# Four score products an item instead of six, in a Macaron layer on one core

## What is computed

```python
x = x + 0.5 * _L0_ffn_ref(_layernorm(x, axis=-1), ...)
x = x + _L0_attn_ref(_layernorm(x, axis=-1), ...)
x = x + 0.5 * _L0_ffn_ref(_layernorm(x, axis=-1), ...)
...
attn = jnp.einsum('bhqd,bhkd->bhqk', q * scale, k)
attn = jnp.where(causal[None, None], attn, -jnp.inf)
attn = jax.nn.softmax(attn, axis=-1)
out = jnp.einsum('bhqk,bhkd->bqhd', attn, v).reshape(b, s, d)
```

## Time and profile before

| | before |
|---|---|
| runs | 1226.78 us median of 3 (1225.18 to 1227.13) |
| profiled execution | 1226.45 us, span in the trace 1224.7 us |
| PE busy | 1165.3 us (95%), weight loads 701.2 us (57%) |
| DVE, ACT, POOL busy | 796.2 (65%), 578.0 (47%), 669.8 us (55%) |
| granted clock of PE | 0.992 of full speed over the span |
| L420, the scores | 192 products, 24.3 us busy |

### The profile page before, as it was taken

The page is one execution under the profiler, slowest core; times in us unless marked ns, Lnnn a source line. Parts: engine busy times, 40 slices in busy tenths (PEclk is TensorE's granted clock), DMA queues, the critical chain, the costliest instruction groups (busy, mean ns, idle before and its releaser), DMA issues.

```text
span 1224.7 us, 22657 instructions
## 1 busy us (share of the span) xinstructions
PE 1165.3 (95%) x8315; PEld 701.2 (57%) x8315; DVE 796.2 (65%) x1571; ACT 578.0 (47%) x954; POOL 669.8 (55%) x740
## 2 busy tenths in 40 slices
PE   4699999998999899999899999899999999999998
PEld 2355555565555566666566566566565565666655
DVE  5688787567866766666766667767567555554444
ACT  3444454343456545555455554554644545333332
POOL 4454334357567766666666677577564546333332
PEclk9799999999999999999999999999999999999999
DMA  6112120000000000000000000000000000000000
GB/s 217 45 56 82 52 65 1 1 1 1 1 1 1 1 1 2 1 1 2 1 2 1 1 1 2 1 18 2 1 2 1 18 1 1 1 10 9 1 1 19
DMA packets 10107, 19.25 MB, mean 16 GB/s; under 512 B 2192, under 2 KB 6800, under 8 KB 10000
## 3 DMA queue, kind: packets, MB, share of 16 engines
q1 hardware_dynamic: 8992, 14.64, 3.7%
q10 hardware_dynamic: 1008, 3.15, 0.7%
HBM read 15.70 MB, written 2.10 MB: 15 GB/s over the span
## 4 chain that ended last, share of the span: by engine, by line
PE 69%; DVE 7%; POOL 3%; issue 2%; ACT 1%; DVEq 0%; ACTq 0%; POOLq 0%
PE YB L297 20%; PE G L278 19%; PE U L278 19%; PE S L420 2%; POOL RR L1067 1%; PE S L446 1%; PE S L461 1%; DVE TS L680 1%; PE S L352 1%; DVE MXN L891 1%; DVE TS L684 1%; ACT TS L509 1%; PE S L392 1%; PE S L396 1%; PE S L398 1%
## 5 line engine op out<-in xcount | busy, mean ns | idle before, releaser
L1011 POOL TENSOR_TENSOR HS<-TS,HS 128x512 f16<-128x512 f32 x256 | 303.1, 1184 | 433.5 <-ACT HS L516 433.1
L680 DVE SCALAR_TENSOR_TENSOR TS<-TS,G 128x512 f32<-128x512 f32 x256 | 175.6, 686 | 372.0 <-ACT TS L509 371.6
L297 PE MATMUL YB<-W,HS 128*128 128x256 f16 x3036 | 374.7, 273 | 20.3 <-DVE X L700 20.3
L278 PE MATMUL G<-XS,W 128*128 128x512 f16 x1536 | 377.5, 382 | 2.9 <-ACT W L523 1.8
L278 PE MATMUL U<-XS,W 128*128 128x512 f16 x1536 | 376.4, 381 | 0.0
L297 PEld LDWEIGHTS YB<-W,HS 128*128 128x128 f16 x3036 | 292.2, 98 | 98.7 <-DVE X L700 29.9
L509 ACT ACTIVATE TS<-G,TSC 128x512 f32<-128x512 f32 x256 | 175.5, 686 | 297.5 <-PE U L278 290.9
L516 ACT ACTIVATE HS<-TS 128x512 f16<-128x512 f32 x256 | 161.2, 630 | 273.8 <-DVE TS L684 268.1
L278 PEld LDWEIGHTS U<-XS,W 128*128 128x128 f16 x1536 | 151.1, 98 | 183.9 <-issue 4.4
L278 PEld LDWEIGHTS G<-XS,W 128*128 128x128 f16 x1536 | 147.6, 98 | 136.4 <-issue 6.4
L684 DVE SCALAR_TENSOR_TENSOR TS<-TS,U 128x512 f32<-128x512 f32 x256 | 175.8, 687 | 8.8
(11 more groups left out here) (160 smaller groups left out, 861.6 us busy)
## 6 DMA issues: line engine op xcount, KB each, us to landing
out_y<-X SPq DMA_DIRECT2D x16, 128.0 KB, 1.7
X<-in_x SPq DMA_DIRECT2D x3, 512.0 KB, 6.1
room<-in_gate SPq DMA_DIRECT2D x3, 512.0 KB, 3.1
room<-in_up SPq DMA_DIRECT2D x3, 512.0 KB, 3.2
room<-in_down SPq DMA_DIRECT2D x3, 512.0 KB, 3.9
QKT<-in_gate SPq DMA_DIRECT2D x3, 512.0 KB, 3.6
QKT<-in_up SPq DMA_DIRECT2D x3, 512.0 KB, 3.7
QKT<-in_down SPq DMA_DIRECT2D x3, 512.0 KB, 4.5
```

Of the source, the lines that this page charges most:

```text
L278: mm = eng.matmul(bank[:, :], W[:, e, wl, jj, kk * I + m * P:kk * I + (m + 1) * P], flat(XS16[:, b % 2, xl, kk, :, :], 'cq'), start=q == 0 ...
L297: mm = eng.matmul(out, HS[:, j % 2, hl, kk, m * P:(m + 1) * P], W[:, e, wl, 2, kk * D:(kk + 1) * D], start=kk + hl + wl == 0, stop=kk == K ...
L680: eng.scalar_tensor_tensor(TS[:, k % 3, :], TS[:, k % 3, :], 1.0, GB[k % 2][:, :], ALU.add, ALU.mult).then_inc(L['v_t'].sem, 1)
L1011: eng.tensor_tensor(HS[:, j % 2, 1, m, :], TS[:, k % 3, :], HS[:, j % 2, 0, m, :], ALU.subtract).then_inc(L['g_lo'].sem, 1)
```

## The change

The scores of an item are laid out anew over the three banks. Before, bank S0 held block a (first keys, first query tile), S1 block b (first keys, second query tile) and S2 block c (second keys, second query tile), each bank filled by both halves of the array, one 256-column product from each; the second product of a bank waited for the first. Now S1 and S0 each take the first keys for both query tiles from one half of the array, a single product of 512 columns each, and only S2 (block c) still takes two products of 256 columns, the second one waiting for the first.

What follows from the layout: blocks a and b now hold both query tiles, and in both the half of the first tile has to be masked. One `pool_mask` does both (a select over 2 x 256 elements a partition, as many as before), and `act_ph` of block b now has to wait for it. `act_ph` b moves from slot s+2 to s+3, and `pool_pl` b from s+3 to s+4. `pe_pv` reads other places of the same blocks, in as many products.

```diff
--- before.py
+++ after.py
@@ -195,7 +195,7 @@
         N_AW = 8
         L = {}
         for name, labels in [
-                ('p_gu', 'gu'), ('p_y', 'y'), ('p_w', 'wt wb'), ('p_lg', 'lg'), ('p_ft', 'tp'), ('p_at', 'tp'), ('p_qt', 'q'), ('p_kt', 'k'), ('p_q2', 'q'), ('p_mx', 'ab'), ('p_qk', 'qkv'), ('p_s0', 'a0 b1 c1'), ('p_sc', 'b a c'), ('p_pv', 'pv'), ('p_op', 'tp mm'),
+                ('p_gu', 'gu'), ('p_y', 'y'), ('p_w', 'wt wb'), ('p_lg', 'lg'), ('p_ft', 'tp'), ('p_at', 'tp'), ('p_qt', 'q'), ('p_kt', 'k'), ('p_q2', 'q'), ('p_mx', 'ab'), ('p_qk', 'qkv'), ('p_s0', 'c0'), ('p_sc', 'b a c'), ('p_pv', 'pv'), ('p_op', 'tp mm'),
                 ('a_t', 'tanh'), ('a_h', 'hi'), ('a_w', 'hi0 hi1 hi2 sc2'), ('a_wq', 'hi'), ('a_fx', 'xh'), ('a_fc', 'xs'), ('a_ac', 'xt'), ('a_qc', 'q'), ('a_kc', 'k'), ('a_q2', 'q'), ('a_rx', 'ex'), ('a_ax', 'xh'), ('a_e', 'b a c'), ('a_ph', 'b a c'), ('a_qh', 'qhi khi0 khi1'), ('a_ot', 'ot'),
                 ('v_t', 't'), ('v_h', 'h'), ('v_y', 'y'), ('v_mx', 'mx0 mx1 mx2'), ('v_wr', 'wr dg'), ('v_sc', 'cl pe rc tsc gu cf sc'), ('v_lo', 'lo0 lo1'), ('v_wq', 'cl pe rc qs sc lo'),
                 ('v_fst', 'stats'), ('v_fag', 'aggr'), ('v_fep', 'eps'), ('v_fx', 'xn'), ('v_ls', 'ls mx sub'), ('v_rp', 'sum rc p eq gt'), ('v_wt', 'cum wt'), ('v_wb', 'wtc'), ('v_wc', 'wc'),
@@ -415,19 +415,18 @@
             s2_read(eng, s)
             eng.wait_ge(*L['a_q2'].at(2 * b + 1, 'q'))
 
-            def part(bank, kt, qt, h):
+            def part(bank, kt, qts, h):
+
                 r = slice(64 * h, 64 * h + 64)
-                return eng.matmul(bank[:, h * 2 * P:(h + 1) * 2 * P], qk[r, kt, H // 2 + kv, :], qk[r, qt, 2 * kv:2 * kv + 2, :], start=(bank is S0) == (h == 0), stop=False, skip_group_check=True, tile_position=(64 * h, 0))
-            part(S0, 0, 0, 0).then_inc(L['p_s0'].sem, 1)
-            part(S1, 0, 1, 1).then_inc(L['p_s0'].sem, 1)
-            part(S2, 1, 1, 1).then_inc(L['p_s0'].sem, 1)
-
-            eng.wait_ge(*L['p_s0'].at(i, 'b1'))
-            part(S1, 0, 1, 0).then_inc(lane.sem, 1)
-            eng.wait_ge(*L['p_s0'].at(i, 'a0'))
-            part(S0, 0, 0, 1).then_inc(lane.sem, 1)
-            eng.wait_ge(*L['p_s0'].at(i, 'c1'))
-            part(S2, 1, 1, 0).then_inc(lane.sem, 1)
+                n = len(qts) * 2 * P
+                out = bank[:, 0:n] if kt == 0 else bank[:, h * n:(h + 1) * n]
+                return eng.matmul(out.rearrange('p (t g q) -> p t g q', t=len(qts), g=2), qk[r, kt, H // 2 + kv, :], qk[r, qts[0]:qts[-1] + 1, 2 * kv:2 * kv + 2, :], start=kt == 0 or h == 0, stop=False, skip_group_check=True, tile_position=(64 * h, 0))
+            part(S2, 1, (1,), 0).then_inc(L['p_s0'].sem, 1)
+            part(S1, 0, (0, 1), 1).then_inc(lane.sem, 1)
+            part(S0, 0, (0, 1), 0).then_inc(lane.sem, 1)
+
+            eng.wait_ge(*L['p_s0'].at(i, 'c0'))
+            part(S2, 1, (1,), 1).then_inc(lane.sem, 1)
 
         def pe_pv(eng, i, s):
             bank = (S0, S0, S1, S2)[i % 4]
@@ -439,11 +438,12 @@
             for qt in range(2):
                 for g in range(G):
                     o = bank[:, (qt * G + g) * VW:(qt * G + g + 1) * VW]
-                    terms = [(0, 0)] if qt == 0 else [(1, 0), (2, 1)]
+
+                    terms = [(g % 2, 2 * qt + g // 2, 0)] + [(2, 2 * (g % 2) + g // 2, 1)] * qt
                     q = 0
-                    for blk, kt in terms:
+                    for blk, at, kt in terms:
                         for ph in (PH, PL):
-                            mm = eng.matmul(o, ph[:, blk, g // 2 + g % 2 * 2, :], VS[:, b % 3, kt, kv, :], start=q == 0, stop=q == 2 * len(terms) - 1)
+                            mm = eng.matmul(o, ph[:, blk, at, :], VS[:, b % 3, kt, kv, :], start=q == 0, stop=q == 2 * len(terms) - 1)
                             q += 1
             mm.then_inc(L['p_pv'].sem, 1)
 
@@ -616,9 +616,7 @@
             if c == 'b':
 
                 eng.wait_ge(*L['p_pv'].at(i - 1, 'pv'))
-                eng.wait_ge(*L['a_e'].at(i, 'b'))
-            else:
-                eng.wait_ge(*L['g_mk'].at(i, c))
+            eng.wait_ge(*L['g_mk'].at(i, 'c' if c == 'c' else 'a'))
             eng.activation(flat(PH[:, blk, :, :], 'gk'), flat(P32[:, blk, :, :], 'gk'), ACT.Copy).then_inc(L['a_ph'].sem, 1)
 
         def act_ot(eng, t):
@@ -648,8 +646,8 @@
                 act_exp(eng, i, 'a')
             for i in due(ITEM, s, 2):
                 act_exp(eng, i, 'c')
+            for i in due(ITEM, s, 3):
                 act_ph(eng, i, 'b')
-            for i in due(ITEM, s, 3):
                 act_ph(eng, i, 'a')
             for i in due(ITEM, s, 4):
                 act_ph(eng, i, 'c')
@@ -1095,9 +1093,9 @@
             eng.tensor_copy(vs[:, :, 2 * HD:3 * HD], VR[:, 1, :, :]).then_inc(lane.sem, 1)
 
         def pool_mask(eng, i, c):
-            blk = 'abc'.index(c)
             eng.wait_ge(*L['a_e'].at(i, c))
-            eng.affine_select(out=P32[:, blk, :, :], in_=P32[:, blk, :, :], compare_op=ALU.is_ge, fill=0.0, base=0, pattern=[[0, G], [1, P]], channel_multiplier=-1).then_inc(L['g_mk'].sem, 1)
+            p, pattern = (P32[:, 0:2, 0:2, :], [[0, 2], [0, 2], [1, P]]) if c == 'a' else (P32[:, 2, :, :], [[0, G], [1, P]])
+            eng.affine_select(out=p, in_=p, compare_op=ALU.is_ge, fill=0.0, base=0, pattern=pattern, channel_multiplier=-1).then_inc(L['g_mk'].sem, 1)
 
         def pool_pl(eng, i, c):
             blk = 'abc'.index(c)
@@ -1122,8 +1120,8 @@
                 pool_mask(eng, i, 'a')
             for i in due(ITEM, s, 3):
                 pool_mask(eng, i, 'c')
+            for i in due(ITEM, s, 4):
                 pool_pl(eng, i, 'b')
-            for i in due(ITEM, s, 4):
                 pool_pl(eng, i, 'a')
             for i in due(ITEM, s, 5):
                 pool_pl(eng, i, 'c')
```

## The result

| | before | after |
|---|---|---|
| median | 1226.95 us (1225.18 to 1227.28, 4 runs) | 1234.49 us (1232.10 to 1235.55, 4 runs) |
| ratio | | 1.0067 (95%: 1.0054 to 1.0079), slower |
| profiled execution, span | 1226.45, 1224.7 us | 1232.10, 1230.3 us |
| from the first score product to the end of the span | 1224.7 - 341.8 = 882.9 us | 1230.3 - 339.7 = 890.6 us |

The last line leaves out the start-up, which differs from one execution to the next (the first score product comes at 338.8 to 342.2 us in the fourteen traces of this study); by it the change costs 7.7 us.

A forecast was written before the change was run, and what follows sets the result against it. PE's own work plus a few stalls bound the kernel. Batches 0, 2, 4 lose 1.8 us, batches 1, 3, 5 lose 6.3, batches 6 and 7 gain 0.36 and 0.48: 7.3 slower, 1234.0 us; range 1226 to 1238.

The forecast's parts named there:

- score block, gain an item: PE's score products: the block takes 0.58 us instead of 0.70, a gain of 0.12 an item, 3.8 us for 32.
- item 18, the power late against its scores: POOL's layer-norm power at item 18 starts 0.96 us later, as DVE's second sine product waits out a POOL operation.
- item 18, loss in an odd batch: The late power passes on fully to PE's scores of item 27: 0.96 us lost.
- item 27, loss in an odd batch: ACT's tanh starts 0.54 us later, DVE's cast falls behind a POOL operation, PE's down product loses 1.63 us.
- an odd batch in all: Batches 1, 3, 5: 4 x 0.12 - 0.96 - 1.63 = -2.11 us each, 6.3 slower.
- batches 2 and 4 in all: Batches 0, 2, 4 alike: 3 x 0.12 - 0.96 = -0.60 us each, 1.8 slower.
- Rival 4: The 512-column score products of the array halves don't overlap: 3.8 gain becomes 2.9 loss, 1240.7 us; chance 0.05.
- The terms put at nothing: Products with the values, exponentials and the mask's walk over 2 x 256 elements were costed at nothing.
- Rival 3: DVE operations beside POOL only slip by 0.3 and 0.54 us, nothing blocks: about no change, 1226.8 us; chance 0.10.
- rival 2: Only one of the two DVE-POOL collisions: without item 18's 1230.1 us, without item 27's 1230.8; chance 0.22.
- Rival 1: Only the scores' gain stays, the delays end in slack: 1223.0 us; chance 0.15.
- Even batches: The late power delays DVE's router operations, ACT's tanh and the addition PE awaits: wait 1.9 us instead of 0.96.

The follow-up runs named there:

- the mask taken early: Mask of block a moved ahead of the layer-norm power on POOL: kernel after 1228.99 us, with block b's remainder back in s+3 too 1226.73, kernel before 1230.52.
- the addition first: DVE's two small operations on the maxima issued behind the addition that PE awaits: kernel after 1222.04 us, with block b's remainder back 1215.24, kernel before 1219.22.

## Why the prediction was right

It said 1234.0 us and the median is 1234.49; the loss after the start-up is 7.7 us where the sum had 7.3. Term by term:

| step | forecast | measured |
|---|---|---|
| score block, gain an item | 0.12 | 0.14 |
| item 18, the power late against its scores | 0.96 | 0.97 |
| item 18, loss in an odd batch | 0.96 | 1.07 |
| item 27, loss in an odd batch | 1.63 | 1.66 |
| an odd batch in all | -2.11 | -2.16 (88.05 to 90.21) |
| batches 2 and 4 in all | -0.60 | -0.68 (91.55 to 92.23, batch 2) |
| batch 0 in all | -0.60 | -0.95 |

- **The scores.** The overlap of the 512-column products was right. The wait was 0.03 too dear: I took the third pair's 0.37, and the fourth product starts at 0.34. Rival 4 is out. The terms put at nothing (the mask's new pattern, the exponentials, the products with the values) show no cost in the count of batch 1.
- **Item 18.** The second sine product behind L1009 (1.18 us long, 0.15 behind its start, 0.18 after its end) and the 0.96 are as said. What was left out is the prediction's own rule that a saving just ahead of a wait is lost: item 18's 0.14 goes into the wait ahead of item 27's scores, which makes the 1.07. Rival 3 and one half of rival 2 needed it to slip in. The wait ahead of item 27's scores was to be 1.3 and is 0.54 + 0.77 = 1.31, part of it now at the down product.
- **Item 27.** The tanh held by both roundings, the cast behind L1009 and the 1.5 stall are as said. The cast took 0.88, and it was 0.34 behind L1009 rather than 0.30. Rival 1 needed this cast in time and fails here.
- **Even batches: the size roughly right, the place wrong.** I put the delay at the addition (0.96 to 1.9). It went to the scores, 0.44 to 1.55, while the addition's wait grew by 0.15. The size came out by luck, in that both places hang on the same late power; PE's waits for the addition rose by 5.1 us and not by the 8 I had named. The list of what the first score product waits for has `v_ls`, DVE's reading of the router's logits, which stands behind the same L871; I had followed the chain through ACT only. Batch 0 went from 432.66 - 341.8 = 90.9 us to 431.50 - 339.7 = 91.8; it lost some 0.25 more than batches 2 and 4 because its wait for ACT's L571, 1.08 us before, takes what items 0 and 9 save. This wait stood in the trace of before, and I had read only the waits for L700 and those ahead of the scores.
- **The sum** is right partly because small errors cancel: two more hundredths saved in each of 32 items (0.6 us) against somewhat more loss in batches 0 to 5.

Open: why the waiting product starts at 0.34 now and started at 0.37 before, although the products waited for are of the same size. Before, its wait was for the block's second product (`b1`), now it is for the first (`c0`); whether this makes the 0.03 no run shows.

## What to carry to other kernels

A saving on the busiest engine is paid only if nothing that moves with it lands in front of an instruction that this engine waits for; write down, for each moved instruction, what starts beside it on VectorE and GpSimd, to a tenth of a microsecond: here a product that came 0.15 us behind the start of a POOL operation was held for 0.86. In this kernel a collision was best mended where it starts to matter: the order in which the awaited instruction stands ahead of those that can be held (one line) made the kernel faster than any shifting of the colliding operations did. A saving just ahead of a wait is lost as well, so go through every wait of the busiest engine, and not only the largest group of them. And after such a repair look at the next place: the mask taken early cured one collision, made two, and made a stall longer behind which the clock could fall.

## What the runs showed of the hardware that was not expected

- The granted clock fell to its lower level directly behind a stall of 2.0 us of PE with busy work around it (twelve products in 1.74 to 2.66 us instead of 1.48) in four of nine such stalls, over the three kernels with the early mask and without the addition first. It did so behind none of the 21 stalls of 1.81 to 1.83 us of seven other kernels. A stall of this size can so cost more than itself, and not each time; that it is the length of the stall that decides is not shown.
- A cast of 128x16, 0.20 us alone, took up to 1.02 us, as long as the POOL operation that it met had left. A tensor_scalar of 128x256 (L839) took 0.41 us alone (372.89 in the trace before), 0.72 beside POOL's mask and 1.24 beside L1011.
- Where PE was held up just ahead of them, the scores start about 1.1 us after the operation that held it has ended, before and after alike: 1.11 behind POOL's L1011, for which the last down product waits, in batch 1, and 1.06 and 1.07 behind DVE's read of the logits in batch 0. Their first product carries a list of twelve waits; whether its length makes the 1.1 us no run shows.
- On PE the view of waits counts less than is lost: 1.54 us of idle time for 1.66 us from start to start, since the ends of products are modelled.
